# A routed network's first ffn1 stores by slot, and its attention gathers rows by token and pads its scores

## The reference

```python
# ffn1: each token goes to its two best of 8 experts
logits = jnp.einsum('bsd,de->bse', x, Wg) + bg
topk_scores, topk_idx = jax.lax.top_k(logits, TOP_K)
topk_scores = jax.nn.softmax(topk_scores, axis=-1)
...
h = jnp.einsum('td,edf->etf', tokens, W1) + b1[:, None, :]
a = jnp.where(even, jax.nn.gelu(h, approximate=False), jax.nn.silu(h))
y = jnp.einsum('etf,efd->etd', a, W2) + b2[:, None, :]
out = jnp.einsum('te,etd->td', comb, y)

# attention: one head, queries and keys of 16, values are the rows themselves
q = jnp.einsum('bsd,ed->bse', x, w_q) + b_q
k = jnp.einsum('bsd,ed->bse', x, w_k) + b_k
scores = jnp.where(mask[None], jnp.einsum('bqe,bke->bqk', q, k) * scale, -10000.0)
out = jnp.einsum('bqk,bkv->bqv', jax.nn.softmax(scores, axis=-1), x)

x = x + 0.5 * ffn1(layernorm(x));  x = x + attention(layernorm(x));  x = x + 0.5 * ffn1(layernorm(x))
```

## Time and profile before

| | |
|---|---|
| median of three runs | 2200.8 us |
| profiled execution | 2198.65 us, span of its records 2196.9 us |
| busy, share of the span | PE 78%, weight loads 65%, DVE 62%, ScalarE 39%, POOL 49% |
| granted clock, mean | 0.868 |
| first ffn1's expert loop | about 1407 to 1652 us |
| attention | about 1658 to 1849 us |

### The profile page before, as it was taken

The page is one execution under the profiler, slowest core; times in us unless marked ns, Lnnn a source line. Parts: engine busy times, 40 slices in busy tenths (PEclk is TensorE's granted clock), DMA queues, the critical chain, the costliest instruction groups (busy, mean ns, idle before and its releaser), DMA issues. The chain is left out here.

```text
span 2196.9 us, 37127 instructions
## 1 busy us (share of the span) xinstructions
PE 1715.4 (78%) x11038; PEld 1421.1 (65%) x11039; DVE 1360.8 (62%) x3041; ACT 846.2 (39%) x1874; POOL 1068.3 (49%) x1178
## 2 busy tenths in 40 slices
PE   6889653999999999999798994476674888376673
PEld 4479641788888888888556993376672556266562
DVE  4535476899999999997553546633443546723435
ACT  2222124555555555554221221343342443234331
POOL 2136443577777767776303552555551001355552
PEclk9989856999999999999799995588985667589987
DMA  6011210000000000000400115011112003111114
GB/s 206 1 27 40 66 41 0 1 1 1 1 1 1 1 1 1 1 1 1 147 22 20 34 37 167 14 40 39 37 36 82 1 1 87 39 39 39 38 37 132
DMA packets 60858, 81.58 MB, mean 37 GB/s; under 512 B 24720, under 2 KB 30896, under 8 KB 60720
## 3 DMA queue, kind: packets, MB, share of 16 engines
q1 hardware_dynamic: 46640, 51.01, 7.4%
q0 software_dynamic: 14080, 28.86, 4.7%
HBM read 54.93 MB, written 24.90 MB: 36 GB/s over the span
## 5 line engine op out<-in xcount | busy, mean ns | idle before, releaser
L820 POOL DMA_INDIRECT y_rows<-y,slot_row x220 | 219.7, 999 | 281.1 <-DVE y L951 134.1
L860 PE MATMUL ps<-w,inner_slot 128*128 x1760 | 262.7, 295 | 94.0 <-DVE y L951 69.5
L860 PEld LDWEIGHTS ps<-w,inner_slot 128*128 128x128 f32 x1760 | 233.6, 206 | 108.8 <-issue 108.1
L848 PE MATMUL ps<-gT,w_slot 128*128 128x128 f32 x1760 | 261.4, 296 | 50.2 <-ACT gT L882 42.2
L848 PEld LDWEIGHTS ps<-gT,w_slot 128*128 128x128 f32 x1760 | 236.8, 209 | 63.6 <-issue 46.2
L928 DVE TENSOR_TENSOR hb<-ps,b 128x512 f32<-128x512 f32 x142 | 98.1, 691 | 271.1 <-PE ps L848 154.5
L1632 DVE SCALAR_TENSOR_TENSOR cv<-ps,cw,cv 128x1021 f32<-128x1021 f32 (+2 forms) x192 | 245.0, 1276 | 12.8 <-ACT cv L1534 10.4
L814 POOL DMA_INDIRECT rows_in<-xn_rows,slot_token x188 | 190.9, 1015 | 69.1 <-issue 50.0
L1812 POOL TENSOR_TENSOR y<-t,sz 128x256 f32<-128x256 f32 x128 | 94.4, 738 | 187.1 <-DVE t L1676 184.1
L1412 PE MATMUL ps<-xnT,win 128*128 128x512 f32 x256 | 131.2, 638 | 21.3 <-DVE cv L1632 17.9
L1461 PE MATMUL ps<-XB,LM 128*128 128x64 f32 x1024 | 142.5, 262 | 0.0
(11 more groups left out here) (281 smaller groups left out, 4205.8 us busy)
## 6 DMA issues: line engine op xcount, KB each, us to landing
w<-in_L_ffn_W SPq DMA_DIRECT2D x6, 2048.0 KB, 10.2
back<-y_rows SPq DMA_DIRECT2D x48, 256.0 KB, 5.5
xn_rows<-xn SPq DMA_DIRECT2D x32, 256.0 KB, 3.5
rows_in<-xn_rows,slot_token POOLq DMA_INDIRECT x220
y_rows<-y,slot_row POOLq DMA_INDIRECT x220
out_x<-x SPq DMA_DIRECT2D x8, 256.0 KB, 3.0
win<-in_L_attn_in_w SPq DMA_DIRECT2D x1, 1544.0 KB, 9.6
b<-in_L_ffn_b SPq DMA_DIRECT2D x2, 512.0 KB, 10.5
```

Of the source, the lines that this page charges most:

```text
L820: nc.gpsimd.indirect_dma_start(kept, bass.IndirectOffsetOnAxis(ap=k.slot_row[:, s:s + 1], axis=0), k.y[:, s % RING, :], None).then_inc(sto ...
L848: ins = nc.tensor.matmul(h1[:, u, b * P:(b + 1) * P], w[:, b * P:(b + 1) * P], k.gT[:, r, :], start=True, stop=True)
L860: ins = nc.tensor.matmul(py[:, q % 2, :], k.inner_slot[:, q % RING, b * P:(b + 1) * P], w_dn[:, ds(e * (FB * D) + b * D, D)], start=(b == ...
```

## The change

In the first ffn1 (the stage that an attention follows) the expert loop's scatter goes away. SP stores each slot's tile plainly at the slot's own place. In the attention the 16 plain loads go away, and POOL gathers the two rows of each token by `k.pos`, with 8 indirect DMAs a group, 64 in all. Its queue is: zeros into bqk; group 0; masks; first half of group 1; deviations 0; second half of group 1; first half of group 2; deviations 1; second half of group 2; then group 3, deviations 2, group 4, deviations 3, and so on.

qT, kT and the projection weights get 128 rows or columns, filled up with zeros; the block order is another; the first score of a batch waits for one group only; in the first batch score(0) stands before project(1). The small loads of weights and biases go from SP to ScalarE's queue. The second ffn1 keeps its scatter.

```diff
@@ experts
-    stored = [k.counter(f"slot_stored{r}", 16, lead=0) for r in range(RING)]
+    stored = [k.counter(f"slot_kept{r}" if by_token else f"slot_stored{r}", 16, lead=0) for r in range(RING)]
...
-                if t >= LEADS:
+                if t >= LEADS and not by_token:
                     scatter(t - LEADS)
...
+        @block.sync
+        def _(sp):
+            if by_token:
+                for s in range(slots):
+                    sp.wait_ge(y_ready.sem, y_ready.at(s + 1))
+                    sp.dma_start(kept[s * P:(s + 1) * P, :], k.y[:, s % RING, :]).then_inc(stored[s % RING].sem, 16)
@@ attend
-    ORDER = (7, 0, 6, 1, 5, 2, 4, 3)
+    ORDER = (3, 2, 7, 1, 6, 4, 5, 0)
+    HALF = P // 2
...
-        wqk, wT, bqk = S("wqk", [QK, 2, D]), S("wT", [P, 2, 32]), S("bqk", [QK, 2])
-        qT, kT = S("qT", [QK, TOK]), S("kT", [QK, TOK])
+        wqk, wT, bqk = S("wqk", [QK, 2, D]), S("wT", [P, 2, HALF]), S("bqk", [P, 2])
+        qT, kT = S("qT", [P, TOK]), S("kT", [P, TOK])
...
+        def ps_p(g):
+            return k.ps[:, 4 if g == 1 else 7, :]
...
-        FIRST, SECOND = {0: 0, 3: 1}, {1: 0, 4: 1}
-        STATISTICS, NORM = {2: 0, 5: 1}, {3: 0, 6: 1}
-        ROWS, PROJECT, PUT = {3: 0, 6: 1}, {4: 0, 7: 1}, {4: 0, 7: 1}
+        FIRST, SECOND = {0: 0, 1: 1}, {0: 0, 2: 1}
+        STATISTICS, NORM = {1: 0, 3: 1}, {2: 0, 5: 1}
+        ROWS, PROJECT = {3: 0, 6: 1}, {4: 0, 7: 1}
@@ sync
-                for dst, src in loads:
-                    sp.dma_start(dst, src, allow_slow_non_contiguous=True).then_inc(weights_in.sem, 16)
-                bring_back(k, sp, 2, back, returned)
@@ gpsimd
+                def fetch(g, c):
+                    for t in range(g * GRP, (g + 1) * GRP):
+                        G.indirect_dma_start(back[:, g, c, t % GRP, :], None, k.y_rows[0:SLOTS2 * P, :],
+                                             bass.IndirectOffsetOnAxis(ap=k.pos[:, c * NT + t:c * NT + t + 1], axis=0)
+                                             ).then_inc(returned[g].sem, 16)
+
+                G.memset(bqk[:, :], 0.0).then_inc(masks.sem, 1)
+                fetch(0, 0)
+                fetch(0, 1)
                 G.affine_select(out=keep[:, :], in_=k.ones[:, :], compare_op=ALU.is_ge, fill=0.0, base=0,
...
+                fetch(1, 0)
+                deviations(0)
+                fetch(1, 1)
+                fetch(2, 0)
+                deviations(1)
+                fetch(2, 1)
+                for g in range(2, NG):
+                    if g + 1 < NG:
+                        fetch(g + 1, 0)
+                        fetch(g + 1, 1)
                     deviations(g)
@@ vector
-                        wait(dve, returned[g], 2)
+                        wait(dve, returned[g], 2 * GRP)
...
+                V.memset(kT[HALF:, :], 0.0).then_inc(zeros.sem, 1)
@@ tensor
-                    nc.tensor.matmul(ps_p[0:64, :], wT[:, :, :].rearrange("p a n -> p (a n)"),
+                    nc.tensor.matmul(ps_p(g), wT[:, :, :].rearrange("p a n -> p (a n)"),
...
-                    if n % QB == 0:
-                        wait(pe, qk_ready, 2 * b + 2)
+                    wait(pe, qk_ready, 2 * b + (1 if n % QB < 2 else 2))
...
-                for g in range(2):
-                    rows(g)
-                    project(g)
+                rows(0)
+                project(0)
+                rows(1)
+                score(0)
+                project(1)
@@ scalar
-                    A.activation(qT[:, cols], ps_p[0:QK, :], ACT.Identity, bias=bqk[:, 0:1])
-                    A.activation(kT[:, cols], ps_p[32:32 + QK, :], ACT.Identity, bias=bqk[:, 1:2]).then_inc(qk_ready.sem, 1)
+                    A.activation(qT[:, cols], ps_p(g), ACT.Identity, bias=bqk[:, 0:1])
+                    A.activation(kT[0:HALF, cols], ps_p(g)[HALF:, :], ACT.Identity, bias=bqk[0:HALF, 1:2]).then_inc(qk_ready.sem, 1)
...
+                for dst, src in loads:
+                    act.dma_start(dst, src).then_inc(weights_in.sem, 16)
+                wait(act, masks, 1)
+                for dst, src in biases:
+                    act.dma_start(dst, src, allow_slow_non_contiguous=True).then_inc(bias_in.sem, 16)
...
-                for g in range(2):
-                    norm(g)
-                    copy_rows(g)
-                    put(g)
+                norm(0)
+                copy_rows(0)
+                norm(1)
+                put(0)
+                copy_rows(1)
+                put(1)
@@ macaron
+                ffn1(k, w, by_token=STAGES[i + 1:i + 2] == ("attn",))
```

More of the change, by code:

```diff
@@ L772, in shared, with experts @@
     close_places(k, NG, 1)
-def experts(k, top, slots, early=0):
+def experts(k, top, slots, early=0, by_token=False):
     nc = k.nc
@@ L992, in attend @@
     SCALE = float(QK) ** -0.5
-    ORDER = (7, 0, 6, 1, 5, 2, 4, 3)
+    ORDER = (3, 2, 7, 1, 6, 4, 5, 0)
     N = BATCH * QB
     TURN, MIX, KEPT = 2, 3, 4
+    HALF = P // 2
     w_turned, w_ready = k.counter("attn_w_turned"), k.counter("attn_w_ready")
-    masks = k.counter("attn_masks")
+    masks, zeros = k.counter("attn_masks"), k.counter("attn_zeros")
     projected, qk_ready = k.counter("attn_projected"), k.counter("attn_qk_ready")
@@ L1006, in attend @@
         k.counter(n) for n in ("prep_var_ready", "prep_rstd_ready", "prep_xn_ready", "prep_transposed", "prep_xt_copied"))
-    returned = back_counters(k)
+    back_counters(k)
+    returned = [k.counter(f"attn_fetched{g}", 16, lead=0) for g in range(NG)]
     assert k.pending == 2
@@ L1019, in attend @@
         x, xn, xnT, stat, mv, rstd = k.x, k.xn, k.xnT, k.stat, k.mv, k.rstd
-        loads = [(wqk[:, 0, :], w["L1_attn_w_q"]), (wqk[:, 1, :], w["L1_attn_w_k"]),
-                 (bqk[:, 0:1], w["L1_attn_b_q"].unsqueeze(1)), (bqk[:, 1:2], w["L1_attn_b_k"].unsqueeze(1))]
+        loads = [(wqk[:, 0, :], w["L1_attn_w_q"]), (wqk[:, 1, :], w["L1_attn_w_k"])]
+        biases = [(bqk[0:QK, 0:1], w["L1_attn_b_q"].unsqueeze(1)), (bqk[0:QK, 1:2], w["L1_attn_b_k"].unsqueeze(1))]
         ps_s = [k.ps[:, 2 * r:2 * r + 2, :].rearrange("p b n -> p (b n)") for r in range(2)]
         ps_t = k.ps[:, 4:6, :].rearrange("p b n -> p (b n)")
-        ps_o, ps_p = k.ps[:, 6, 0:D], k.ps[:, 7, :]
+        ps_o = k.ps[:, 6, 0:D]
+        def ps_p(g):
+            return k.ps[:, 4 if g == 1 else 7, :]
         def block_of(n):
@@ L1066, in deviations @@
                     G.tensor_scalar(shift[:, r, :], shift[:, r, :], -1.0, None, ALU.mult).then_inc(rstd_ready.sem, 1)
+                def fetch(g, c):
[6 more added lines that the diff above has]
+                fetch(0, 1)
                 G.affine_select(out=keep[:, :], in_=k.ones[:, :], compare_op=ALU.is_ge, fill=0.0, base=0,
                                 pattern=[[-1, P]], channel_multiplier=1).then_inc(masks.sem, 1)
-                wait(pool, masks, 1)
+                wait(pool, masks, 2)
                 G.tensor_scalar(fill[:, :], keep[:, :], -1.0, 10000.0 / SCALE, ALU.add, ALU.mult).then_inc(masks.sem, 1)
-                for g in range(NG):
+                fetch(1, 0)
[8 more added lines that the diff above has]
+                        fetch(g + 1, 1)
                     deviations(g)
@@ L1107, in maximum @@
                     if n == 0:
-                        wait(dve, masks, 2)
+                        wait(dve, masks, 3)
                     V.tensor_tensor(last, last, keep[:, :], ALU.mult).then_inc(own.sem, 1)
@@ L1160, in score @@
                     b, q, t = block_of(n)
-                    if n % QB == 0:
-                        wait(pe, qk_ready, 2 * b + 2)
+                    wait(pe, qk_ready, 2 * b + (1 if n % QB < 2 else 2))
+                    if n == 0:
+                        wait(pe, zeros, 1)
                     wait(pe, expd, n - 1)
@@ L1262, in _ @@
                             norm(group_behind(NORM, n))
-                            copy_rows(group_behind(NORM, n))
-                        if group_behind(PUT, n) is not None:
-                            put(group_behind(PUT, n))
+                        if group_behind(ROWS, n) is not None:
+                            copy_rows(group_behind(ROWS, n))
+                        if group_behind(PROJECT, n) is not None:
+                            put(group_behind(PROJECT, n))
         weights_in.close(len(loads))
+        bias_in.close(len(biases))
         for s in (scored, summed, maxed, expd, turned, pt_ready, mixed, added):
@@ L1272, in attend @@
         w_ready.close(2)
-        masks.close(2)
+        masks.close(3)
+        zeros.close(1)
         for s in (projected, qk_ready, stat_own, var_ready, rstd_ready, xn_ready, transposed, xt_copied):
@@ L1276, in attend @@
         pool_own.close(3 * NG)
-        close_back(k, 2, returned)
+        k.first_added.close(NG)
+        k.added.close(NG)
+        for s in returned:
+            s.close(2 * GRP)
 def mamba(k, w):
@@ L1997, in macaron @@
         setup(k, w)
-        for stage in STAGES:
```

(8 more changed lines are left out.)

21 lines of the change are left out of this document (12 added, 9 removed).

## The result

| | before | after |
|---|---|---|
| median, same chip | 2200.84 us (4 runs) | 2114.61 us (4 runs) |
| ratio, 95% interval | | 0.9587 [0.9548, 0.9626] |
| profiled execution (span) | 2198.65 us (2196.9) | 2124.94 us (2123.2), the slowest of its four |

I forecast 2169 in a range of 2156 to 2192. The change gains 86 us, the forecast had 32. The direction was right; the largest term of the gain is one that I had put at 0, the first ffn1's scatter.

What follows compares the result with a forecast made beforehand. The prediction took the attention to be bound by PE, and PE by its clock. It summed -1 for the store and -28.7 for the attention to about -30, from 2198.65 to 2169 us, range 2156 to 2192.

Steps and rivals of the forecast that it cites:

- The scatter at 0: First ffn1's expert loop: replacing the scatter by SP's plain store leaves the loop's length unchanged, 0 us.
- The attention: Attention stage: 29 us a batch from the second on, ending at 161.5 us instead of 190.2, so -28.7 us.
- the later gathers: POOL's attention gathers, 16 per batch: 20 us, with deviations 24 of 29 us, covered unless one takes over 1.55 us.
- The clock: Attention's padded scores and projections: granted clock about 1.0 from the second batch on, bounds 0.69 and 1.00.
- Rival (C): Attention: padding does nothing for the clock, late start of 13 us stays; 2204 us, chance 0.10.
- The late start: Attention's start: POOL's queue of gathers makes the third block 13.2 us late, of which 10 come back by exp(8).
- (B): Attention: clock rises, but DVE and the chain bound batches at 34 us each; 2183 us, chance 0.17.
- (E): Attention: DVE hides fully under PE, 26.5 us a batch, start 3 us faster; 2161 us, chance 0.08.
- (D): Attention: gathers cost more and POOL's queue sets the end; at 2.5 us each 2226 us, chance 0.05.
- The store's tail (-1): End of the first ffn1: the store leaves right behind the last y, gaining at most 1.95 us, taken as -1.

## Why the prediction was wrong, step by step

**The scatter at 0: the step that failed.** I read that POOL was busy 140 of 247 us and waited 66 us for y, and that nobody waited long for a gathered tile, and concluded that "the loop's length hangs on PE, ScalarE and DVE and stays: 0 us". It measured -77 us (226.9 to 149.9). The loop has no resource that is full: PE has 166 of 227 us [the row of the loop before, above]. That should have been the question, since nothing in my sum explained the other 61. What fills them stands in the timeline of before, one slot of it:

```profile
1549.70 1.06 PE L848 MATMUL ps<-gT,w_slot 128*128 128x128 f32 x8
...
1550.57 1.17 POOL L814 DMA_INDIRECT rows_in<-xn_rows,slot_token  x1 [0.30 <-issue]
...
1552.04 0.99 POOL L820 DMA_INDIRECT y_rows<-y,slot_row  x1 [0.30 <-issue]
...
1553.34 0.97 POOL L814 DMA_INDIRECT rows_in<-xn_rows,slot_token  x1 [0.30 <-issue]
...
1555.42 0.69 DVE L928 TENSOR_TENSOR hb<-ps,b 128x512 f32<-128x512 f32 x1 [4.32 <-PE ps L848]
```

and in the loop's waits, before and then after:

```profile
DVE hb L928 <- PE ps L848: 63.8, 34, 4.3
...
DVE hb L928 <- remote: 53.3, 15, 5.3
```

```profile
DVE hb L937 <- PE ps L857: 39.1, 47, 1.6
```

DVE adds the bias 4.7 us behind the recorded end of the matmuls that it waits for (1550.76; they are the 43rd set of the loop, and this is the 43rd addition), and the profile shows nothing else that it waits for; "remote" is a wait whose end no record explains. The waits of this one addition fall from 117.1 to 39.1 us. PE then stands still, and its clock is lower: 0.88 before, 0.99 after.

The same can be counted for all 71 slots of any run: how long behind the recorded end of its matmuls each addition starts.

| chips | indirect DMAs a slot on POOL | mean lateness |
|---|---|---|
| quick | 1, 1.5 or 2 | 0.15 to 0.18 us |
| slow | 1 gather | 0.23 to 0.36 us |
| slow | 1 scatter | 0.51 us |
| slow | 1.5 | 1.16 us |
| slow | 2 | 1.68 to 1.93 us |

DVE is not what is late. The trace also has the times at which PE's signal for a set was recorded, for most of the slots, and the addition starts 0.13 us (median) behind the last of them, before and after alike.

That the cause on slow chips is the indirect DMAs on POOL is shown by the runs with one more and with every other one (216 and 177 us), by the plain store on POOL (149.6), by the plain load in place of the gather (164.4) and by POOL busy without a DMA (149.0). On quick chips there is none of it (at most 0.18 us on average), and the 27 us there are POOL's time to issue (2.46 us a slot, 174.5 us for 71). Through what an indirect DMA delays PE's results is open: the profile models the ends of matmuls, so late ends and late signals look alike, and why chips differ in it no run here tells.

**The attention: right in its shape, 5 to 7 us off at the end.** First exponential predicted at 40 us, 39.8 and 39.3 in the two executions; third 51.4, 51.2 and 51.3; ninth 77, 77.0 and 77.3. From the second batch on I took 29 us: the third took 29.1 and 29.7, but the second 34.8 and 36.0. While it ran, POOL issued fetches (18.7 us busy there, 3.3 in the next); with plain loads the second took 28.2, and with the fetches on a quick chip 29.4. This looks like the effect of the loop; the lateness was not counted here. The end came at 166.0 and 168.1, against 161.5; on quick chips it came at 158. Against the stages before (184 to 190 us) the gain is 16 to 24 us where I had 28.7, and the run with the attention alone gained only 9 to 12 of the whole. Gathers in a row stood 1.25 us apart, as taken; the 1.55 us at which the later gathers would no longer be covered were not reached.

**The clock.** I took about 1.0 for padded scores; 0.91, 0.94 and 1.00 in the batches. Rival (C) had padding do nothing: refuted by 0.72 against 0.94 at the same work in the third batch, and by 0.95 there in the order of before.

**The late start** was priced at 13.2 us of which 10 come back. Against the start of before that is so (77 to 74.0). But the price of the fetches is to be read against the same order and padding with plain loads, and there it is 27 us at the ninth exponential. The absolute times were right, and what the fetches cost was hidden in them.

**(B), (E), (D)** did not come. The store's tail (-1): the gap between last y and first step of the attention is 9.1 us where it was 8.4, nothing gained.

**What the text said would refute it** was a shorter loop, "which would mean the scatter had been holding y". The loop was shorter; the reason attached to it is wrong too, since the extra gather holds no y.

## What to carry to other kernels

When no engine fills a loop, the time between is a term of its own: find its largest wait and compare its end with the record that should have ended it before costing a removed step at nothing. Where a plain DMA will do in place of an indirect one, try it, and count the indirect ones that stay per loop step: here the store by slot gained 27 us on one kind of chip and 77 on the other, and the fetches behind it took about 30 back. Measure a price against the same kernel without the item, not against the old kernel.

## What the runs showed of the hardware that I had not expected

- Chips differ, or their condition does: the kernel before takes 2063 to 2064 us on two and 2193 to 2213 on three. ffn1's loops with two indirect DMAs a slot take 174 to 175 us on the first and 226 to 237 on the others; with one gather a slot both take 148 to 150.
- On a slow chip an extra indirect gather costs 0.8 to 0.9 us of a loop beside PE work that doesn't use it, and DVE gets PE's results later (1.2 to 1.9 us behind their recorded end instead of 0.3); 0.97 us of POOL memset per slot costs nothing (loop 149.0 us), and neither does a plain store issued by POOL (149.6 us).
- The same count of matmuls, with the scores' contraction filled up from 16 to 128 rows and the projection from 64 to 128 columns by zeros, runs in the attention's third batch at 0.94 to 0.95 of the full clock instead of 0.69 to 0.85.
